# FFN's first batch moved into the last steps of attention 0, and x loaded one step later

## The reference, cut to what matters

```python
    h = _layernorm(x, axis=-1) * (1 + ca) + sa
    x = x + ga * _L0_attn_ref(h, ...)           # 16 heads of width 8, latent k and v
    h = _layernorm(x, axis=-1) * (1 + cb) + sb
    x = x + gb * _L0_ffn_ref(h, ...)
def _L0_ffn_ref(x, ...):                        # w1, w2, h1, h2, w3 are ternary
    h = _silu(_tlin(x, w1_w, w1_s)) * _tlin(x, w2_w, w2_s)      # u
    h = gelu(_tlin(h, h1_w, h1_s))
    h = gelu(_tlin(h, h2_w, h2_s))
    return _tlin(h, w3_w, w3_s)
```

## Time and profile before

| | |
|---|---|
| median of 3 runs | 847.55 us (847.18 to 848.71) |
| profiled execution, its own time | 842.6 us |
| its span | 840.5 us |
| mean granted TensorE clock | 0.954 |
| PE busy | 724.7 us (86%) |
| DVE busy | 631.7 us (75%) |
| ACT busy | 540.2 us (64%) |
| POOL busy | 384.2 us (46%) |
| attention 0: first maxima, last addition to x | 29.54 us, 306.71 us |
| FFN: first instruction, first matmul of h1 | 308.34 us, 319.27 us |

### The profile page before, as it was taken

One profiled execution on the slowest core, in us unless ns is written; L12 is line 12 of the kernel. 1 busy time (PEld: TensorE's weight loads), 2 busy tenths in 40 slices (PEclk: granted clock), 3 DMA queues, 4 the chain that ended last, 5 costly groups with the idle time before them and its releaser, 6 DMA issues. The chain is left out here.

```text
span 840.5 us, 17121 instructions
## 1 busy us (share of the span) xinstructions
PE 724.7 (86%) x5737; PEld 505.9 (60%) x5737; DVE 631.7 (75%) x1426; ACT 540.2 (64%) x1195; POOL 384.2 (46%) x482
## 2 busy tenths in 40 slices
PE   5668899989998857889999997589998968999996
PEld 3323333334333336888999997467776756788874
DVE  3668988878988826778777763378889749988885
ACT  3126677767776735688788885288887734655553
POOL 6244455445442001421220000689998634766664
PEclk9999999989999976999999999599999879999999
DMA  3765555553453003000000000000000161544430
GB/s 92 105 123 81 94 72 68 75 62 61 72 74 40 4 17 127 1 1 1 2 1 1 2 1 1 2 2 2 2 2 1 47 159 50 153 127 123 125 103 25
DMA packets 76423, 44.18 MB, mean 53 GB/s; under 512 B 6144, under 2 KB 74160, under 8 KB 76208
## 3 DMA queue, kind: packets, MB, share of 16 engines
q1 hardware_dynamic: 76336, 43.07, 26.7%
HBM read 27.83 MB, written 2.25 MB: 36 GB/s over the span
## 5 line engine op out<-in xcount | busy, mean ns | idle before, releaser
L593 DVE TENSOR_REDUCE att_negmax<-att_p_max 128x2 f32<-128x512 f32 x256 | 170.4, 688 | 35.2 <-PE att_p_max L473 33.0
L694 ACT ACTIVATE att_probs<-att_p_sT 128x1024 f32<-128x1024 f32 x128 | 130.8, 1025 | 61.3 <-PE att_p_sT L479 58.5
L473 PE MATMUL att_p_max<-att0p_QK 48*128 48x256 bf16 x512 | 103.4, 293 | 27.5 <-DVE att_negmax L593 16.0
L2114 POOL TENSOR_TENSOR moe_z_lo<-moe_z,moe_z_hi 128x512 fp32r<-128x512 f32 x64 | 94.2, 1481 | 55.1 <-ACT moe_z_hi L2049 48.0
L479 PE MATMUL att_p_sT<-att0p_QK 51*128 51x256 bf16 x512 | 100.0, 281 | 0.6 <-ACT att_probs L694 0.3
L473 PEld LDWEIGHTS att_p_max<-att0p_QK 48*128 48x128 bf16 x512 | 29.1, 96 | 109.2 <-DVE att_negmax L593 55.7
L989 POOL TENSOR_TENSOR ffn0s_rstd<-ffn0s_var_eps,top_minus_half 128x2 f32<-128x2 f32 x16 | 11.6, 724 | 179.8 <-DVE ffn0s_var_eps L976 179.8
L943 PE MATMUL ffn0s_p_h<-ffn0s_u_hi,top_ffn_all 128*128 128x256 f32 x256 | 70.9, 309 | 16.5 <-DVE ffn0s_u_lo L1204 16.2
L501 PE MATMUL att_p_o<-att_probs,att0p_V 128*32 128x256 f32 x1024 | 83.1, 398 | 0.5 <-ACT att_probs L694 0.5
L1204 DVE TENSOR_TENSOR ffn0s_g_lo<-ffn0s_g,ffn0s_g_hi 128x512 fp32r<-128x512 f32 x64 | 48.7, 776 | 41.9 <-ACT ffn0s_g_hi L1148 40.7
L2093 DVE TENSOR_TENSOR moe_z<-moe_act_u,top_ffn_all 128x512 f32<-128x512 f32 x64 | 77.0, 1203 | 2.2
(11 more groups left out here) (248 smaller groups left out, 1954.2 us busy)
## 6 DMA issues: line engine op xcount, KB each, us to landing
top_ffn_all<-combine SPq DMA_DIRECT2D x32, 512.0 KB, 6.8
att0p_QK<-att_parts SPq DMA_DIRECT2D x192, 64.0 KB
att_raw<-in_L_ffn_h_w SPq DMA_DIRECT2D x8, 256.0 KB, 4.2
out_x<-top_X SPq DMA_DIRECT2D x8, 256.0 KB, 2.3
top_X<-in_x SPq DMA_DIRECT2D x2, 768.0 KB, 9.1
top_wo_all<-gates SPq DMA_DIRECT2D x4, 256.0 KB, 4.5
top_gbo_all<-gates SPq DMA_DIRECT2D x4, 256.0 KB, 5.2
top_wo_all<-gates SPq DMA_DIRECT2D x1, 1024.0 KB, 7.1
```

What stands on the lines that cost most here:

```text
L473: mm = pe.matmul(bank(at)[:, i, :], QK[r][rows, g, 0, i * P:(i + 1) * P], QK[r][rows, g, 1, :], start=True, stop=True)
L593: dve.tensor_reduce(negmax[:, :, w, g], bank(at)[:], AX.X, ALU.max, negate=True).then_inc(drained, 1)
L694: act.activation(probs[g % 2][:, t % 2], p_sT[t % 2][:], ACT.Exp).then_inc(exped, 1)
L2114: pool.tensor_tensor(z_lo[e % RING][:], z[e % RING][:], z_hi[e % RING][:].bitcast(F32), ALU.subtract).then_inc(z_lo_ready, 1)
```

## The change

It has two parts.

**The tail.** FFN's work on batch 0, from the layer norm to both parts of u, is put into slots of steps 18 to 20 of attention 0 (`pe_head`, `act_head`, `dve_head`), with the layer norm of batch 1 up to xn and the statistics of batch 2. Banks, buffers and semaphores that both phases use are made once, ahead of both (`ffn_shared`): `p_ab` serves as attention 0's `p_sT` and as FFN's `p_a` and `p_b`, and `p_m` is one bank for both. Since the flag isn't there yet, batch 0 takes the program of three matmuls. FFN's own block begins with the turn of batch 1 and with h1 of batch 0. Buffers move to make room: `wmod` and the raw weights lie in `k.wide`, which later holds tanh, gated, u and hT, and still later `k.beats`; FFN's h and the first u lie in `k.h_hi`.

**The head.** Parts 2 and 3 of x are issued in steps 2 and 3 instead of 1 and 2. The products of the modulation are split: `pe_second` after step 0, `pe_third` after step 1, `pe_turn_gates` after step 2. The gates are stored at the end of step 3 instead of step 1 and read back at the start of steps 4 to 7, ahead of the copies of `sp_stack`, instead of the end of steps 2 to 5. POOL's bias moves from step n-3 to n-5 and its gating of weights from n-3 to n-4. The fill of QK's rows of ones for buffers 2 and 3 comes before the modulation on VectorE instead of after it.

```diff
         def pe_turn_back(pe, b):
             pe.wait_ge(drained, RING["O", b] + 1)
             pe.wait_ge(v_ready, min(b + 5, B))
+            if b == B - 2:
+                pe.wait_ge(f.h_hi_ready, 1)
...
+        def pe_head(pe, n, slot):
+            if (n, slot) == (B + 2, 9):
+                pe.wait_ge(maxT_ready, B)
+                f.ln.pe_turn(pe, 0, p_m)
+            if (n, slot) == (B + 3, 8):
+                pe.wait_ge(w_lo_ready, WEIGHT_GROUPS)
+                pe.wait_ge(exped, PAIRS * (B - 1) + PAIRS - 1)
+                f.pe_a(pe, 0, 0, 0, False)
+                f.pe_b(pe, 0, 0, 0, False)
+            if (n, slot) == (B + 3, 11):
+                pe.wait_ge(exped, PAIRS * B)
+                f.pe_a(pe, 0, 0, 1, False)
+            if (n, slot) == (B + 3, 14):
+                f.pe_b(pe, 0, 0, 1, False)
+
+        def act_head(act, n, slot):
+            if (n, slot) == (B + 2, 10):
+                act.wait_ge(c.gbo_ready, 1)
+                f.act_h(act, 0, 0)
+            if (n, slot) == (B + 3, 8):
+                act.wait_ge(scales_ready, 3)
+                f.act_tanh(act, 0, 0)
+            if (n, slot) == (B + 3, 10):
+                f.act_tanh(act, 0, 1)
+            if (n, slot) == (B + 3, 12):
+                f.act_u_hi(act, 0, 0, 0)
+            if (n, slot) == (B + 4, 2):
+                f.act_u_hi(act, 0, 0, 1)
+
+        def dve_head(dve, n, slot):
+            if (n, slot) == (B + 2, 3):
+                dve.wait_ge(drained, RING["out", 2] + 1)
+                f.ln.dve_stats(dve, 0)
+            if (n, slot) == (B + 2, 5):
+                f.ln.dve_normalise(dve, 0)
+            if (n, slot) == (B + 2, 10):
+                f.ln.dve_stats(dve, 1)
+            if (n, slot) == (B + 2, 12):
+                f.dve_h_lo(dve, 0, 0)
+            if (n, slot) == (B + 2, 13):
+                f.ln.dve_normalise(dve, 1)
+            if (n, slot) == (B + 3, 1):
+                f.ln.dve_stats(dve, 2)
+            if (n, slot) == (B + 3, 9):
+                dve.wait_ge(scales_ready, 3)
+                f.dve_u(dve, 0, 0, 0)
+            if (n, slot) == (B + 3, 15):
+                f.dve_u(dve, 0, 0, 1)
+                f.dve_u_lo(dve, 0, 0, 0)
+            if (n, slot) == (B + 4, 2):
+                f.dve_u_lo(dve, 0, 0, 1)
...
+        def sp_gates(sp, c):
+            of = slice(c * GATES, (c + 1) * GATES)
+            if c == 0:
+                sp.wait_ge(gates_stored, 16)
+            at_least(sp, gates_loaded, 32 * c)
+            for to, kind in ((k.wo1_all, 0), (k.gbo1_all, 1)):
+                sp.dma_start(to[:, of, :], k.gates_dram[of, kind, :].rearrange("(o b) d -> o b d", o=1).to_broadcast([P, GATES, D])
+                             ).then_inc(gates_loaded, 16)
+
         def sp_step(sp, n):
+            if 0 <= n - 4 < B // GATES:
+                sp_gates(sp, n - 4)
             if batch_valid(n - 1):
                 sp_stack(sp, n - 1, (n - 1) % NB, 0)
                 sp_stack(sp, n - 1, (n - 1) % NB, 1)
@@
-            if n in (1, 2):
-                c.sp_x(sp, n + 1)
-            if n == 1:
+            if n in (2, 3):
+                c.sp_x(sp, n)
+            if n == 3:
                 sp.wait_ge(gate_rows_ready, 1)
                 sp.dma_start(k.gates_dram, gate_rows[:]).then_inc(gates_stored, 16)
-            if n == 2:
-                sp.wait_ge(gates_stored, 16)
-            if 0 <= n - 2 < B // GATES:
...
@@ pool_step
-            if batch_valid(n - 3):
-                pool_bias(pool, n - 3)
-            if 0 <= n - 3 < B // GATES:
-                pool_gate_wo(pool, n - 3)
+            if batch_valid(n - 5):
+                pool_bias(pool, n - 5)
+            if 0 <= n - 4 < B // GATES:
+                pool_gate_wo(pool, n - 4)
@@ POOL's program of attention 0
-            for n in range(B + 3):
+            for n in range(LAST):
                 pool_step(pool, n, n % NB)
...
+            for b in range(HEAD):
+                f.ln.pool_rstd(pool, b)
@@ TensorE's
             for n in range(LAST):
                 pe_step(pe, n, n % NB)
+                if n == 0:
+                    c.pe_second(pe)
                 if n == 1:
-                    c.pe_rest(pe)
+                    c.pe_third(pe)
+                if n == 2:
                     pe_turn_gates(pe)
@@ VectorE's
                 if n == 0:
                     c.dve_ones(dve, 1)
                     c.dve_v_ones(dve, 1)
+                    c.dve_ones(dve, 2)
                 if n == 1:
+                    c.dve_ones(dve, 3)
                     for r in (2, 3):
                         c.dve_v_ones(dve, r)
                     c.dve_mod_rest(dve)
-                    for r in (2, 3):
-                        c.dve_ones(dve, r)
@@ ffn0, TensorE's program
-            for n in range(WHOLE0):
+            ln.pe_turn(pe, 1, p_m)
+            for n in range(2, WHOLE0):
                 pe_step(pe, n, n % 2, exact)
```

More of the change, by code:

```diff
@@ L292, in ffn_weight_loads @@
     groups = []
+    raw = [of.rearrange("p m q -> p (m q)") for of in raw]
     for name, ob, ib, at in FFN_PLAN:
@@ L345, in attention0 @@
         OTn = sb("OTn", [P, S])
-        raw = [sb(f"raw{n}", [P, F]) for n in range(3)]
+        raw = f.early_raw
         lo_sums = sb("lo_sums", [P, 4])
@@ L549, in pe_step @@
                     pe_out(pe, y)
[L550 to L557, removed]
+                if slot == PES["ln"] and batch_valid(fill):
+                    pe_ln(pe, fill)
+                if slot == PES["q"] and batch_valid(fill):
+                    pe_q(pe, fill)
+                if slot == PES["k"] and batch_valid(fill):
+                    pe_k(pe, fill)
+                if slot == PES["v"] and batch_valid(fill):
+                    pe_v(pe, fill)
                 if slot == PES["O"] and batch_valid(t):
@@ L630, in dve_step @@
         def dve_step(dve, n):
-            f, m, s, t, y = n, n - 2, n - 3, n - 4, n - 5
+            fill, m, s, t, y = n, n - 2, n - 3, n - 4, n - 5
             for slot in range(TILES):
@@ L649, in dve_step @@
                     dve_max_tile(dve, m, slot)
-                if slot == DVE["stats"] and batch_valid(f + 1):
-                    dve_stats(dve, f + 1)
+                if slot == DVE["stats"] and batch_valid(fill + 1):
+                    dve_stats(dve, fill + 1)
+                dve_head(dve, n, slot)
         def act_hT(act, b):
@@ L731, in act_step @@
                     act_exp(act, t, (TILES - SCORES + slot) // 2)
+                act_head(act, n, slot)
         def sp_max(sp, b, r):
@@ L1282, in _ @@
         def _(pool):
-            ln.pool_rstd(pool, 0)
-            for b in range(1, B):
+            for b in range(HEAD, B):
                 ln.pool_rstd(pool, b)
@@ L1318, in _ @@
         def _(act):
-            for n in range(WHOLE0):
+            f.act_h(act, 1, 1)
+            for n in range(2, WHOLE0):
                 act_step(act, n, n % 2)
@@ L1328, in _ @@
         def _(dve):
-            ln.dve_stats(dve, 0)
-            ln.dve_normalise(dve, 0)
-            for n in range(WHOLE0):
+            f.dve_h_lo(dve, 1, 1)
+            ln.dve_normalise(dve, 2)
+            for n in range(2, WHOLE0):
                 dve_step(dve, n, n % 2)
```

265 lines of the change are left out of this document (147 added, 118 removed).

## The result

The change took the median from 847.37 to 823.04 us: a ratio of 0.9715, with a 95% interval of 0.9686 to 0.9743. I had forecast 846.5, with a range of 839.5 to 851.0. It is faster by far more than I expected, and the time is outside the range. In a second set on another chip the same kernel had 823.59 against 844.10, a ratio of 0.9814 (0.9761 to 0.9867). Ratios and their intervals leave out the slow runs of a kernel (more than 1.5% above its fastest) and medians take in all, so that here and there the two differ by some tenths of a per cent. The profiled execution took 822.84 us, its span is 820.5, 20.0 less than before.

What follows compares the result with a forecast made beforehand. PE, busy 86% of the span, was taken to bound most of attention 0, waiting at head and tail. Head +4.6 and tail −5.6 summed to −1.0: 846.5 us for the median, range 839.5 to 851.0.

Steps and rivals of the forecast that it cites:

- The copies of batch 1 "keep their 15.6": Head, SP's queue: batch 1's copies, with part 2 of x now behind them, still take 15.6 us; step 3 starts at 43.2.
- 11.9 from start to release: Head, step 4: PE gets past slot 8 11.9 us after SP starts the copies of batch 3.
- The copies of batch 0 without x behind them, −2.0: Head: without x queued behind them the first copies land at 27.6, not 29.52, a gain of 2.0 us.
- The hold by the store, copies of batch 3 at 61.2: Head: gate reads wait on SP for the store, so batch 3's copies start at 61.2 instead of 58.1.
- rival D: Head: store lands only with all of part 3 of x, batch 3's copies from 63.4; 850.2 to 851.3; chance 0.18.
- 60.2: Head: when the gates' store lands, taken between 56.7 (its own row's 3.1) and 62.3 (x's 9.1).
- What the hold does to PE, +1.6: Head, slot 8 of step 4: PE idles 4.6 us instead of 1.07 and goes at 73.6, 1.6 later.
- the spell, +3.0: Head, behind PE's 4.6 us idle in step 4: a stretch at 1.2 GHz costing 3.0 us, between 1.7 and 4.4.
- The tail, −9.2 + 3.6: End of attention 0: h1 starts 3.0 us after the last addition, gaining 9.2; extra work costs attention 0 3.6; sum −5.6.
- C: Rival: store lands in 3.1 us beside part 3, SP isn't held, head keeps its 2.0 gain; 839.9 us; chance 0.15.

Runs made afterwards that it cites:

- `head_only`: Kernel before with the head part of the change alone, every buffer where it was: 844.69 us, ratio 1.0002.
- `head_aligned`: Kernel before with the head part of the change and QK at a multiple of 256 bytes, no tail: 827.70 us, ratio 0.9813.
- `before_aligned`: Kernel before with 160 unused bytes per partition ahead of QK, so QK begins at a multiple of 256, parts 160 past one: 828.61 us, ratio 0.9849.
- `destination_moved`: Kernel before with QK moved to a multiple of 256 bytes and the parts kept at one: 828.60 us, ratio 0.9818.
- `tail_aligned`: Changed kernel with the head part undone and QK where the change put it, at a multiple of 256: 824.82 us, ratio 0.9841.

## Why the prediction was wrong, by its own steps

**The copies of batch 1 "keep their 15.6", and "11.9 from start to release".** This is the step that failed. I took the price of a copy from the rows of before and asked only when copies are issued and what lies beside them. Those of batch 1 took 12.5 (13.1 with the place alone, 16.1 in `head_only`), since their destination had moved to a multiple of 256. The diff showed that buffers move; I read the moves as making room. Everything that hangs on the copies went with it: the wait at slot 8 of step 3 (4.09 to 0.93), the waits of steps 7 to 16 (5.3 in all to none, so that steps 7 to 15 take 14.9 to 15.2, where steps 7 to 10 and 12 to 15 took 14.7 to 15.8), and the late copies of step 11 with their spell at the lower clock (21.1 us to 14.9). By the experiments the place alone is worth 15.7 us by the medians (844.32 to 828.61), 12.7 by the ratio (7.3 to 18.2).

**The copies of batch 0 without x behind them, −2.0.** Right in kind, too large. Place for place they took 14.4 instead of 15.7 (`head_only`), and 12.7 instead of 13.6 (`head_aligned`): 1.3 and 0.9. (768 KB, by the way, is three eighths of x, not a quarter.)

**The hold by the store, copies of batch 3 at 61.2.** With slow copies it was there, and longer: 63.09, where rival D had 63.4. I had set two bounds, the store's "own row" of 3.1 and the landing of x, and chosen between them. They are one. The issues of 22 to 29 us in the kernel before hold one part of x and the store, and so do those of 47 to 50 with the change and of 53 to 55 in `head_only`; in this order:

```profile
top_X<-in_x SPq DMA_DIRECT2D x1, 768.0 KB, 8.8
gates<-att_gate_rows SPq DMA_DIRECT2D x1, 24.0 KB, 3.1
```

```profile
top_X<-in_x SPq DMA_DIRECT2D x1, 768.0 KB, 4.7
gates<-att_gate_rows SPq DMA_DIRECT2D x1, 24.0 KB, 4.4
```

```profile
top_X<-in_x SPq DMA_DIRECT2D x1, 768.0 KB, 8.0
gates<-att_gate_rows SPq DMA_DIRECT2D x1, 24.0 KB, 7.7
```

With the starts on SP's queue, x landed at 31.06 and the store at 31.25; at 52.74 and 52.92; at 61.85 and 62.02. In 14 of the 17 traces the store lands 0.17 to 0.25 behind x. In the other three, `before_aligned`, `destination_moved` and `tail_aligned`, x had 0.4 to 0.5 left when the store was issued, and the store took 1.5. So the 3.1 was no time of a store either, but the rest of x. The trace agrees with the rule of the Trainium skill's page "DMA: Bandwidth & Descriptors" (Queues, rings and completion order) that I gave to rival D: a semaphore's increment lands only after every earlier write of that DMA engine. D's mechanism was the right one, and my 60.2 between two bounds the wrong reading. In the changed kernel the hold is short since its x took 4.7: 49.03 to 52.93.

**What the hold does to PE, +1.6, and the spell, +3.0.** Wrong with slow copies and with quick ones. I had read 11.9 from the copies' start to PE's release as the copies' price. The 9.4 of `head_only` shows that part of it was PE not being there yet. No wait, and so no +1.6. Of the two idle times that I had seen slow tiles behind, the 4.09 of step 3 doesn't count: the tiles there were slow anyway (see the last section). The fall of the clock came in another place: from 91.2 to 104.8, in step 6, which took 21.6. In the 4.1 us ahead of it VectorE was busy 4.0 and PE 2.75, which points to VectorE as what held PE, and not to a copy. PE was idle ahead of the fall, as I had it, but by short waits and not by one of 4.6. It wasn't tried what would remove them.

**The tail, −9.2 + 3.6.** Both held in the changed kernel. h1 starts 2.60 after the end of the last addition (3.0), in each of the six traces with the tail within 0.01: a gain of 9.5. From step 17's first tile to the last addition it is 41.3 instead of 37.3: +4.0 (3.6); over all traces 36.9 to 37.4 without the tail, and 40.1 to 44.2 with it, so the loss runs from 2.7 to 7.4. The reciprocal of O in step 18 begins 26.3 after step 17's start (283.16), not 23.5: 2.8 late, where I had 3.0. From h1's start to FFN's last product it takes 205.5 instead of 204.6; over all traces that is 203.1 to 207.7 without the tail and 203.9 to 206.1 with it, so no third term is shown. By time the tail is worth 3.5 with slow copies by its ratio (−7.3 to +0.3). With quick copies it is 3.8 by the medians (828.61 to 824.82, on two chips) and 0.7 by the ratios (0.9849 to 0.9841). I had 5.6; the runs are too few to tell these apart.

**The rivals.** None of them was what happened. C comes nearest in its sign and its head ("all of the head's 2.0 is kept"), for a reason that it doesn't name: the store didn't land in 3.1. D had the hold right and its effect on PE wrong. All four took the copies' price as fixed.

## What to carry to other kernels

A change that adds or moves a buffer moves all that are allocated behind it. Compare the start addresses of whatever a DMA writes, before and after, as you compare the order of instructions; if the same packets take another time in a stretch where nothing was edited, look there first. Rows of 512 bytes that a copy writes into SBUF are best begun at a multiple of 256 bytes: here it cost 160 unused bytes and one line. Where a pipeline waits a few tenths per step for its copies, as here, a small gain on them may pay more than its size; 64 and 192 bytes past point that way and don't prove it. And when a small DMA seems to take long, look at when the large one in front of it lands.

## What the runs showed of the hardware

- Copies from SBUF to SBUF in packets of 512 bytes (two kinds of place, 17 traces) kept the DMA engines busy 37 to 39% of the steady stretch with a destination at a multiple of 256 bytes, and 52 to 58% with one that began 32, 64, 96, 128 or 192 bytes past it. A source 160 bytes past cost nothing that shows. The quick places were odd multiples of 256 (102144 and 133888), so a multiple of 512 isn't needed, and one of 128 isn't enough.
- Slow packets slow others: part 2 and 3 of x, 768 KB each, landed in 9.0 to 10.2 beside slow copies and in 6.5 to 6.7 beside quick copies, both with the order of before (medians of the two, eleven traces).
- A store of 24 KB landed 0.17 to 0.25 behind the 768 KB issued before it, whether it was issued 0.5 or 5.9 us after them (14 traces). Where these had 0.4 to 0.5 left, it took 1.5 (three traces).
- The granted clock at the head: its row reads 1.00 from the start, but until 57.0 with the change and 63.4 before (57 to 69 over all traces) the tiles last 0.37 to 0.42, and 0.28 afterwards. The trace's first entry on the clock is the rise at that moment, so the row's 1.00 ahead of it is no reading. By the tiles (0.41 in the spell from 182.9 on) the clock was at its lower level, 1.2 GHz. I had taken the 0.37 in step 3 for the effect of its wait.
